# Recurrent mix on one core: the head sums one row further behind, the token sum and the token mix at another row

## The chip, the cores and the metric

The program runs on one core of one Trainium2 chip. The metric is device time in microseconds (us), from launch to end, lower is better. The kernel before takes 2801.14 us, the median of 3 runs (2800.57 to 2802.79).

The program is a chain of eight layers (delta attention, ternary FFN, relative attention, hashed FFN, recurrent mix, low-rank FFN, rotary attention, routed FFN) with a layernorm behind each. The change lies in one of them, the recurrent mix, which takes some 210 us of the span.

## The reference, cut to what matters

The recurrent mix works on 4 batches of 256 tokens in the reference's own shape; the kernel holds the same data as 4 batches of 512 tokens by 128 channels, with a layout of its own. What is computed:

```python
xx  = shifted(x) - x                      # token before, minus token
xxx = x + xx * time_maa_x
m   = tanh(xxx @ time_maa_w1)             # 4 groups of 32
mw, mk, mv, mr = m[f] @ time_maa_w2[f]
xw, xk, xv, xr = (x + xx * (time_maa_f + m_f))
r, k, v = xr @ W_r, xk @ W_k, xv @ W_v
w = time_decay + tanh(xw @ time_decay_w1) @ time_decay_w2
def step(S, (r_t, k_t, v_t, w_t)):        # for each token
    kv = k_t (x) v_t
    y_t = r_t . (S + u * kv)
    return exp(-exp(w_t)) * S + kv, y_t
y = layernorm(y) * ln_g + ln_b
out = y @ W_o
```

The result is added to x, and the program's own layernorm follows.

## The kernel before

Channels lie on the 128 partitions and 512 tokens along the free dimension. There are 4 batches, b = 0 to 3. The state of a head is 16 x 16; its second index is taken apart into HS = 16 passes, here called **rows**: for row j of batch b the kernel scans, along the 512 tokens, the state of all 128 (head, index) pairs against value channel j of their head. The rows of the whole layer are numbered g = 16 b + j, 0 to 63. One row goes through these steps:

- **spread(g)** on TensorE (L922): a 128x512 f32 matmul copies value channel j of each head to the head's partitions, into one of 4 banks of PSUM (g mod 4). It waits for scan g-4, which read that bank last.
- **product(g+1)** and **scan(g)** on VectorE (L1098 and L1106). VectorE issues the product of the next row ahead of the scan of this one.
- **read(g)** on GpSimd (L1065): receptance times state, into one of DEEP = 4 buffers. It waits for sum g-4, which read that buffer last.
- **sum(g)** on TensorE (L929): a matmul that gathers the row into one accumulated bank of PSUM, SUMS, for all 16 rows of the batch. The first sum of a batch (g = 16 b) starts that bank anew, and waits until VectorE has taken the last batch out of it.

TensorE's program is written out by hand: in row j it issues spread(g), then pieces of the next batch's projections and of the last batch's norm, then sum(g - BEHIND), with BEHIND = 3.

Around the rows lie the pieces. For the **next** batch VectorE computes the shifted difference xx and behind it the **token mix** xxx (L1073 and L1075, both in `shift`, row 0). TensorE multiplies it (`tokens_mixed`, L872, row 4), ScalarE takes tanh (L997), TensorE makes the four mixes in two pairs (`first_mixes`, row 6, `later_mixes`, row 8, both L875), VectorE applies them (`scale_mix`, L1079, rows 4 and 6; `add_tokens`, L1083, rows 5, 7 and 8), and TensorE makes values, keys, receptance and decay (L891, L895, L900, L906, L910, L914, rows 10 to 15). For the **last** batch VectorE adds the accumulated sums to a term of its own, the **token sum** (`sum_up`, L1111, row 2), TensorE makes the mean (L935, row 7) and the variance (L939, row 9), VectorE centres and scales (L1116 row 5, L1121 row 9, L1125 row 10), and TensorE and VectorE finish with L945 and L1129 in row 15.

Each engine runs its list in order; semaphores tie the engines together. No DMA and nothing of SyncE's queue takes part in these rows, and no scheduler moves anything: the order is that of the code. The functions below are printed with the line numbers of the profile.

Of the kernel before, what the change touches and what calls it, by code (L numbers as in the profile page):

```python
# [809 lines left out]
def rwkv_attention(c):  # L810
# [4 lines left out]
    d = c.dram  # L815
    HS = 16
    DEEP = 4
    BEHIND = 3
    loaded, chain = c.sem("rw_loaded"), c.sem("rw_chain")
    pe_done, act_done = c.sem("rw_pe"), c.sem("rw_act")  # L820
    spreads, keyed, scanned, read, summed = (c.sem("rw_" + n) for n in ("spreads", "keyed", "scanned", "read", "summed"))
# [1 line left out]
    with ExitStack() as ctx:  # L823
# [41 lines left out]
        def _(eng):  # L865
# [11 lines left out]
            def first_mixes(b):  # L877
                eng.wait_ge(act_done, b * ACTS + 1)
                eng.wait_ge(chain, b * STEPS)
                mix_of(b, 2, 0)  # L880
                mix_of(b, 1, 1)
# [75 lines left out]
            for b in range(B):  # L957
                following, tail = b + 1 < B, b > 0
                for j in range(HS):
                    g = b * HS + j  # L960
                    spread_row(g)
                    if following and j == 4:
                        tokens_mixed(b + 1)
                    if following and j == 6:
                        first_mixes(b + 1)
                    if tail and j == 7:
                        mean(b - 1)
                    if following and j == 8:
                        later_mixes(b + 1)
                    if tail and j == 9:  # L970
                        variance(b - 1)
                    if following and j == 10:
                        values(b + 1)
                    if following and j == 11:
                        keys(b + 1)
                    if following and j == 12:
                        receptance(b + 1)
                        decay_down(b + 1)
                    if following and j == 14:
                        decay_up(b + 1)  # L980
                    if following and j == 15:
                        own_weights(b + 1)
                    if tail and j == 15:
                        output(b - 1)
                    if g >= BEHIND:
                        sums(g - BEHIND)
            for g in range(B * HS - BEHIND, B * HS):
                sums(g)
# [78 lines left out]
        @block.vector  # L1067
        def _(eng):
            def x(b):
                return c.X[:, b, PAD:PAD + T]  # L1070

            def shift(b):
                eng.tensor_tensor(xx[:, :], c.X[:, b, PAD - 1:PAD + T - 1], x(b), ALU.subtract).then_inc(chain, 1)  # L1073
                eng.wait_ge(chain, b * STEPS + 1)
                eng.scalar_tensor_tensor(xxx[:, :], xx[:, :], maa[:, 0:1], x(b), ALU.mult, ALU.add).then_inc(chain, 1)  # L1075

            def scale_mix(b, f, at):
                eng.wait_ge(pe_done, b * PES + at)
                eng.scalar_tensor_tensor(mix[:, f, :], turn(at), maa[:, 1 + f:2 + f], xx[:, :], ALU.add, ALU.mult).then_inc(chain, 1)  # L1079

            def add_tokens(b, f, after):
                eng.wait_ge(chain, b * STEPS + after)
                eng.tensor_tensor(mix[:, f, :], mix[:, f, :], x(b), ALU.add).then_inc(chain, 1)  # L1083

            def own_keys(b):
                eng.wait_ge(act_done, b * ACTS + 4)
                eng.scalar_tensor_tensor(ruk[:, :], rkv[:, b % 2, 2, :], maa[:, 6:7], rkv[:, b % 2, 0, :], ALU.mult, ALU.mult).then_inc(chain, 1)

            def own_values(b):
                eng.wait_ge(pe_done, b * PES + 11)  # L1090
                eng.tensor_tensor(we[:, b % 2, :], rkv[:, b % 2, 1, :], turn(1), ALU.mult).then_inc(chain, 1)

            def products(g):
                b = g // HS
                if g % HS == 0:
                    eng.wait_ge(act_done, b * ACTS + 3)
                eng.wait_ge(spreads, g + 1)
                eng.tensor_tensor(row(g), rkv[:, b % 2, 0, :], row(g), ALU.mult).then_inc(keyed, 1)  # L1098

            def scan(b, j):  # L1100
                g = b * HS + j
                eng.wait_ge(act_done, b * ACTS + 7)
                eng.wait_ge(keyed, g + 1)
                if g >= DEEP:
                    eng.wait_ge(read, g - DEEP + 1)
                eng.tensor_tensor_scan(S[:, j % DEEP, 1:], wd[:, b % 2, :], row(g), 0.0, ALU.mult, ALU.add).then_inc(scanned, 1)  # L1106

            def sum_up(b):
                eng.wait_ge(summed, (b + 1) * HS)
                eng.wait_ge(chain, (b + 1) * STEPS)  # L1110
                eng.tensor_tensor(Y[:, :], we[:, b % 2, :], SUMS, ALU.add).then_inc(yo, 1)  # L1111

            def centre(b):
                eng.wait_ge(ym, b + 1)
                eng.wait_ge(yo, 2 * b + 1)
                eng.tensor_tensor(centred[:, :], Y[:, :], TAIL, ALU.subtract).then_inc(yc, 1)  # L1116

            def scale_norm(b):
                eng.wait_ge(yl, 2 * b + 2)
                eng.wait_ge(yc, b + 1)  # L1120
                eng.scalar_tensor_tensor(own[:, :], centred[:, :], maa[:, 7:8], Q[:, 1, :], ALU.mult, ALU.mult).then_inc(yn, 1)  # L1121

            def shift_norm(b):
                eng.wait_ge(yn, 2 * b + 1)
                eng.tensor_scalar(Y[:, :], own[:, :], maa[:, 8:9], None, ALU.add).then_inc(yn, 1)  # L1125

            def residual(b):
                eng.wait_ge(yr, b + 1)
                eng.tensor_tensor(c.R[:, b, :], x(b), TAIL, ALU.add).then_inc(yo, 1)  # L1129

            for n in range(DEEP):
                eng.memset(S[:, n, 0:1], 0.0)
            eng.wait_ge(loaded, 16 * len(pairs))
            shift(0)
            scale_mix(0, 2, 2)
            scale_mix(0, 1, 3)
            add_tokens(0, 2, 3)
            scale_mix(0, 3, 4)
            scale_mix(0, 0, 5)
            add_tokens(0, 1, 4)  # L1140
            add_tokens(0, 3, 6)
            add_tokens(0, 0, 7)
            own_keys(0)
            own_values(0)
            products(0)
            for b in range(B):
                following, tail = b + 1 < B, b > 0
                for j in range(HS):
                    if b * HS + j + 1 < B * HS:
                        products(b * HS + j + 1)  # L1150
                    scan(b, j)
                    if following and j == 0:
                        shift(b + 1)
                    if tail and j == 2:
                        sum_up(b - 1)
                    if following and j == 4:
                        scale_mix(b + 1, 2, 2)
                        scale_mix(b + 1, 1, 3)
                    if tail and j == 5:
                        centre(b - 1)  # L1160
                    if following and j == 5:
                        add_tokens(b + 1, 2, 3)
                    if following and j == 6:
                        scale_mix(b + 1, 3, 4)
                        scale_mix(b + 1, 0, 5)
                    if following and j == 7:
                        add_tokens(b + 1, 1, 4)
                        add_tokens(b + 1, 3, 6)
                    if following and j == 8:
                        add_tokens(b + 1, 0, 7)  # L1170
                    if tail and j == 9:
                        scale_norm(b - 1)
                    if tail and j == 10:
                        shift_norm(b - 1)
                    if following and j == 12:
                        own_keys(b + 1)
                    if tail and j == 15:
                        residual(b - 1)
                    if following and j == 15:
                        own_values(b + 1)  # L1180
            sum_up(B - 1)
            centre(B - 1)
            scale_norm(B - 1)
            shift_norm(B - 1)
            residual(B - 1)
# [462 lines left out]
def relative_attention(c):  # L1648
# [23 lines left out]
    LAST = NITER * QT  # L1672
    AHEAD, BEHIND, STAGES, RING = 5, 2, 3, 6
    LEAD = AHEAD * QUAD
# [29 lines left out]
    with ExitStack() as ctx:  # L1704
# [120 lines left out]
        def _(eng):  # L1825
# [79 lines left out]
            for j in range(AHEAD):  # L1905
                write_bands(j)
                if j == 0:
                    pack(1)
                elif j <= AHEAD - BEHIND:
                    read_windows(j - 1)  # L1910
# [4 lines left out]
            for j in range(LAST):  # L1915
                m, t = j // QT, j % QT
                if j + AHEAD - BEHIND < LAST:
                    read_windows(j + AHEAD - BEHIND)
# [1318 lines left out]
```

## Time and profile before

| what | value |
|---|---|
| median of 3 runs | 2801.14 us (2800.57 to 2802.79) |
| the profiled execution's own time | 2805.52 us |
| its span | 2803.7 us |
| mean granted TensorE clock | 0.94 |
| TensorE matmul busy over the span | 2424.5 us (86%) |
| VectorE busy over the span | 2077.3 us (74%) |
| ScalarE busy | 1585.5 us (57%) |
| GpSimd busy | 269.5 us (10%) |

The rows of the recurrent mix run from 2126.9 to 2301.3 us of the span, with some 20 us of first projections ahead and a tail behind. "Idle before" in the rows further down is the time in which an engine had nothing running ahead of an instruction, with the instruction that ended the wait. An instruction of VectorE starts some 0.1 us before the profile shows the end of the one ahead of it, so distances from start to start are a little shorter than durations.

### The profile page before, as it was taken

The page shows a single profiled execution, that of the slowest core. Times are in us where ns is not written, and L with a number is a line of the kernel's source. Part 1 is how long each engine was busy: PE and PEld are TensorE (multiplying, and loading weights), DVE is VectorE, ACT ScalarE, POOL GpSimd, SP SyncE. Part 2 cuts the span into 40 slices and gives each one's busy share as a digit, 9 for nine tenths or more (in the row PEclk, how much of TensorE's full clock was granted, in tenths as well). Part 3 has the DMA queues.
Part 4 walks back from the last instruction along what each step waited for, and adds up shares of the span by engine and source line. Part 5 has one row for each costly group of instructions (what it writes and reads, how often), then busy time and mean ns, then how long its engine had stood idle before and what let it go on. Part 6 is the DMA issues. An engine that isn't in the chain of part 4 may idle for free. (4 is left out here: it accounts for less than half of the span.)

```text
span 2803.7 us, 64145 instructions
## 1 busy us (share of the span) xinstructions
PE 2424.5 (86%) x25861; PEld 1600.8 (57%) x25861; DVE 2077.3 (74%) x3811; ACT 1585.5 (57%) x4086; POOL 269.5 (10%) x278
## 2 busy tenths in 40 slices
PE   6888888888888888888994999999998887999777
PEld 5666676666666676674442666666642332332376
DVE  6899898899999989892124777788727775886465
ACT  3566666666667666665334777777641113667344
POOL 0000000000000000000011101100003342110342
PEclk9999999999999999999996999999999998999889
DMA  5111111110111111002007998999510003220421
GB/s 188 32 33 25 25 32 33 32 32 18 32 32 33 33 32 32 17 17 72 0 12 198 229 250 227 229 244 236 130 37 2 0 0 108 70 74 20 176 70 65
DMA packets 205727, 219.50 MB, mean 78 GB/s; under 512 B 32966, under 2 KB 191446, under 8 KB 199990
## 3 DMA queue, kind: packets, MB, share of 16 engines
q1 hardware_dynamic: 202400, 209.59, 28.5%
q0 software_dynamic: 2400, 4.95, 0.5%
q8 instruction: 207, 3.39, 0.5%
q10 hardware_dynamic: 633, 0.85, 0.1%
q14 instruction: 87, 0.71, 0.1%
HBM read 137.96 MB, written 79.79 MB: 78 GB/s over the span
## 5 line engine op out<-in xcount | busy, mean ns | idle before, releaser
L3003 DVE TENSOR_REDUCE dl_ZO<-dl_XP 128x64 f32<-128x128 f32 (+6 forms) x448 | 219.7, 491 | 15.4
L2116 ACT ACTIVATE da_AB<-ps 128x384 f32<-128x384 f32 x256 | 124.7, 491 | 137.7 <-PE ps L1963 134.1
L2578 PE MATMUL ps<-dl_ST,ident 128*128 128x512 f32 x416 | 187.8, 595 | 0.0
L2998 DVE TENSOR_TENSOR dl_XP<-dl_ZO,dl_G 128x128 f32<-128x128 f32 (+5 forms) x384 | 177.1, 461 | 13.2
L1596 DVE TENSOR_REDUCE ra_top<-ps 128x1 f32<-128x512 f32 x256 | 159.2, 680 | 36.1 <-PE ps L1362 35.2
L2126 ACT ACTIVATE da_E<-ps,da_top 128x512 f32<-128x512 f32 x256 | 176.2, 688 | 15.3 <-DVE da_top L2273 14.8
L2270 DVE TENSOR_TENSOR ps<-ps,da_window 128x192 f32<-128x192 f32 (+1 forms) x256 | 101.2, 395 | 111.5 <-PE ps L1986 107.2
L2273 DVE TENSOR_REDUCE da_top<-ps 128x1 f32<-128x512 f32 x256 | 177.0, 691 | 8.8
L1496 ACT ACTIVATE ra_PT<-ps 128x512 f32<-128x512 f32 x256 | 136.0, 601 | 61.0 <-PE ps L1393 60.7
L1993 PE MATMUL ps<-ident,da_E 128*128 128x128 f32 x1024 | 168.7, 288 | 1.3 <-ACT da_E L2126 1.3
L2512 PEld LDWEIGHTS ps<-X,dl_taps_v 128*128 128x128 f32 x1088 | 140.3, 210 | 16.6 <-issue 10.9
L1727 POOL MEMSET da_K<- 32x4096 f32 x2 | 7.0, 3506 | 1456.6 <-POOLq L195 1456.6
L2512 PE MATMUL ps<-X,dl_taps_v 128*128 128x128 f32 x1088 | 142.8, 293 | 4.5 <-DVE dl_taps_v L3061 4.5
L1993 PEld LDWEIGHTS ps<-ident,da_E 128*128 128x128 f32 x1024 | 108.2, 141 | 50.3 <-issue 39.3
L2808 ACT ACTIVATE dl_bv<-dl_Wb,dl_beta_now 128x32 f32<-128x32 f32 x512 | 112.9, 335 | 41.3 <-DVE dl_Wb L2895 39.6
L2816 ACT ACTIVATE dl_FB<-dl_F,dl_beta_now 128x32 f32<-128x32 f32 x512 | 126.8, 350 | 4.0 <-DVE dl_F L2900 2.9
L2512 PE MATMUL ps<-X,dl_taps_q 128*128 128x128 f32 x1088 | 125.9, 274 | 0.0
L2512 PE MATMUL ps<-X,dl_taps_k 128*128 128x128 f32 x1088 | 124.2, 273 | 0.0
L2785 ACT ACTIVATE dl_WT<-ps 128x256 f32<-128x256 f32 x64 | 21.1, 381 | 181.3 <-PE ps L2601 181.3
L2512 PEld LDWEIGHTS ps<-X,dl_taps_q 128*128 128x128 f32 x1088 | 122.8, 191 | 1.1
L2512 PEld LDWEIGHTS ps<-X,dl_taps_k 128*128 128x128 f32 x1088 | 122.8, 191 | 0.0
L2578 PEld LDWEIGHTS ps<-dl_ST,ident 128*128 128x128 f32 x416 | 74.6, 190 | 78.7 <-issue 71.7
(416 smaller groups left out, 5932.2 us busy)
## 6 DMA issues: line engine op xcount, KB each, us to landing
da_bands<-da_AB SPq DMA_DIRECT2D x128, 384.0 KB, 3.8
dl_Abc<-dl_ends SPq DMA_DIRECT2D x64, 512.0 KB, 6.3
da_window<-da_bands SPq DMA_DIRECT2D x128, 192.0 KB, 4.4
da_across<-da_bands SPq DMA_DIRECT2D x128, 192.0 KB, 4.4
da_parts<-da_split SPq DMA_DIRECT2D x64, 96.0 KB, 3.4
ra_parts<-ra_split SPq DMA_DIRECT2D x16, 384.0 KB, 3.7
rf_We<-in_rf_We SPq DMA_DIRECT2D x1, 4608.0 KB, 22.8
da_K<-da_parts SPq DMA_DIRECT2D x16, 256.0 KB
```

Of the source, the lines that this page charges most:

```text
L1496: eng.activation(PT[:, k % 2, h, :], ps[:, tscore_bank(UNITS * m + v), :], ACT.Exp).then_inc(s["exps"], 1)
L1596: eng.tensor_reduce(top[:, m % 2, u:u + 1], ps[:, score_bank(UNITS * m + u), :], AXX, ALU.max, negate=True).then_inc(s["maxima"], 1)
L1993: mm = eng.transpose(ps[:, 2 + U % 2, k * P:(k + 1) * P], E[:, U % 2, k * P:(k + 1) * P], c.ident[:, :])
L2116: eng.activation(AB[:, j % STAGES, h, :, :], ps[:, band_bank(v), 0:2 * BAND].rearrange("p (k x) -> p k x", k=2), ACT.Copy)\
L2126: eng.activation(E[:, U % 2, :], ps[:, score_bank(U), :], ACT.Exp, bias=top[:, u:u + 1], accum_out=total[:, m % 2, u:u + 1]).then_inc(s["e ...
L2273: eng.tensor_reduce(top[:, u:u + 1], bank, AXX, ALU.max, negate=True).then_inc(s["maxima"], 1)
L2512: mm = eng.matmul(out, taps[w][:, tap, cols], columns_of(c.X, m, tap), start=tap == 0, stop=tap == TAPS - 1)
L2578: eng.matmul(ps[:, UPDATES[r], :], c.ident[:, :], quarters[:, r, :, :], start=True, stop=alone)
L2808: ins = eng.activation(bv[:, e, :, t], values[:, t, :], ACT.Copy, scale=beta_now[:, 0, t:t + 1])
L2816: ins = eng.activation(FB[:, e, :, t // SB, t % SB], F[:, e, :, t // SB, t % SB], ACT.Copy, scale=beta_now[:, 1, t:t + 1])
L2998: link(eng.tensor_tensor(XP[:, :, :, SB - t:], seen.unsqueeze(1).to_broadcast([P, 2, I, t + 1]), G[:, x:x + 2, keys][:, ::-1, :].unsqueeze ...
L3003: link(eng.tensor_reduce(ZO[:, to:to + 1 + (2 * I - 1) * CH:CH].rearrange("p (k i) -> p k i", k=2), XP[:, :, :, SB - 1 - t:], AXX, ALU.add))
```

## The change

BEHIND goes from 3 to 4: in row j TensorE now issues sum(g-4) where it issued sum(g-3). The pieces `tokens_mixed`, `first_mixes`, `mean`, `later_mixes` and `variance` go one row later on TensorE; those of rows 10 to 15 stay. On VectorE the token mix is split off from the shifted difference and issued in row 1, and the token sum goes from row 2 to row 1, ahead of the token mix. No instruction is added or taken out.

```diff
-    BEHIND = 3
+    BEHIND = 4
...
                     spread_row(g)
-                    if following and j == 4:
+                    if following and j == 5:
                         tokens_mixed(b + 1)
-                    if following and j == 6:
+                    if following and j == 7:
                         first_mixes(b + 1)
-                    if tail and j == 7:
+                    if tail and j == 8:
                         mean(b - 1)
-                    if following and j == 8:
+                    if following and j == 9:
                         later_mixes(b + 1)
-                    if tail and j == 9:
+                    if tail and j == 10:
                         variance(b - 1)
                     if following and j == 10:
                         values(b + 1)
...
             def shift(b):
                 eng.tensor_tensor(xx[:, :], c.X[:, b, PAD - 1:PAD + T - 1], x(b), ALU.subtract).then_inc(chain, 1)
+
+            def mix_tokens(b):
                 eng.wait_ge(chain, b * STEPS + 1)
                 eng.scalar_tensor_tensor(xxx[:, :], xx[:, :], maa[:, 0:1], x(b), ALU.mult, ALU.add).then_inc(chain, 1)
...
             shift(0)
+            mix_tokens(0)
...
                     if following and j == 0:
                         shift(b + 1)
-                    if tail and j == 2:
+                    if tail and j == 1:
                         sum_up(b - 1)
+                    if following and j == 1:
+                        mix_tokens(b + 1)
```

TensorE at the start of batch 0, from its first spreads on (L922 is a spread, L929 a sum, L872 the tokens' product), before:

```order
L922 MATMUL ps<-rw_rkv,rw_spread 128x512 x4
L929 MATMUL ps<-rw_rS,rw_gather 128x512
L922 MATMUL ps<-rw_rkv,rw_spread 128x512
L872 MATMUL ps<-rw_xxx,rw_w 128x512
L929 MATMUL ps<-rw_rS,rw_gather 128x512
```

and changed:

```order
L922 MATMUL ps<-rw_rkv,rw_spread 128x512 x5
L929 MATMUL ps<-rw_rS,rw_gather 128x512
L922 MATMUL ps<-rw_rkv,rw_spread 128x512
L872 MATMUL ps<-rw_xxx,rw_w 128x512
L929 MATMUL ps<-rw_rS,rw_gather 128x512
```

Five spreads stand ahead of the first sum instead of four. From there on the list reads alike up to the middle of the batch, with every spread one row further on than its neighbours: the tokens' product, which stood behind spread 4, stands behind spread 5.

TensorE in the middle of batch 1, from the mean (L935) by the later mixes (L875) and the variance (L939) to the values (L891), before:

```order
L935 MATMUL ps<-rw_Y,ones_mean 128x512
L929 MATMUL ps<-rw_rS,rw_gather 128x512
L922 MATMUL ps<-rw_rkv,rw_spread 128x512
L875 MATMUL ps<-rw_m,rw_w 128x512 x2
L929 MATMUL ps<-rw_rS,rw_gather 128x512
L922 MATMUL ps<-rw_rkv,rw_spread 128x512
L939 MATMUL ps<-rw_Q,ones_mean 128x512
L929 MATMUL ps<-rw_rS,rw_gather 128x512
L922 MATMUL ps<-rw_rkv,rw_spread 128x512
L891 MATMUL ps<-rw_mix,rw_Wrkv 128x512
```

and changed:

```order
L935 MATMUL ps<-rw_Y,ones_mean 128x512
L929 MATMUL ps<-rw_rS,rw_gather 128x512
L922 MATMUL ps<-rw_rkv,rw_spread 128x512
L875 MATMUL ps<-rw_m,rw_w 128x512 x2
L929 MATMUL ps<-rw_rS,rw_gather 128x512
L922 MATMUL ps<-rw_rkv,rw_spread 128x512
L939 MATMUL ps<-rw_Q,ones_mean 128x512
L891 MATMUL ps<-rw_mix,rw_Wrkv 128x512
```

The variance and the values now stand in one row, with no sum and no spread between them.

VectorE where batch 1 begins, from the shifted difference (L1073) on, before:

```order
L1073 TENSOR_TENSOR rw_xx<-X 128x512
L1075 SCALAR_TENSOR_TENSOR rw_xxx<-rw_xx,rw_maa,X 128x512
L1098 TENSOR_TENSOR ps<-rw_rkv,ps 128x512
L1106 SCALAR_TENSOR_TENSOR rw_S<-rw_wd,ps 128x512
L1098 TENSOR_TENSOR ps<-rw_rkv,ps 128x512
L1106 SCALAR_TENSOR_TENSOR rw_S<-rw_wd,ps 128x512
L1111 TENSOR_TENSOR rw_Y<-rw_we,ps 128x512
L1098 TENSOR_TENSOR ps<-rw_rkv,ps 128x512
```

and changed, where L1100 is the product, L1108 the scan, L1113 the token sum and L1077 the token mix:

```order
L1073 TENSOR_TENSOR rw_xx<-X 128x512
L1100 TENSOR_TENSOR ps<-rw_rkv,ps 128x512
L1108 SCALAR_TENSOR_TENSOR rw_S<-rw_wd,ps 128x512
L1113 TENSOR_TENSOR rw_Y<-rw_we,ps 128x512
L1077 SCALAR_TENSOR_TENSOR rw_xxx<-rw_xx,rw_maa,X 128x512
L1100 TENSOR_TENSOR ps<-rw_rkv,ps 128x512
```

One product and one scan (row 1) stand between the difference and the token sum now, where it was two of each and the token mix; the token mix comes behind the token sum. GpSimd's and ScalarE's lists keep their order.

## Rows read from the trace of the kernel before

**Rows 1.** Windows: length; busy PE, PEld, DVE, ACT, POOL; granted clock; DMA share, GB/s.
```profile
2126.90:2168.40 41.50, 37.04 (x85) 13.76 (x83) 37.36 (x45) 4.30 (x7) 20.08 (x16) 1.00 0.00 0
2168.40:2187.00 18.60, 13.41 (x27) 5.15 (x26) 12.40 (x15) 0.60 (x1) 6.63 (x6) 0.82 0.00 0
2187.00:2218.60 31.60, 29.90 (x69) 11.60 (x68) 28.65 (x36) 8.21 (x11) 14.37 (x11) 1.00 0.00 1
2218.60:2237.60 19.00, 13.22 (x25) 5.11 (x25) 12.28 (x15) 0.60 (x1) 6.29 (x5) 0.82 0.00 0
...
2269.20:2301.30 32.10, 27.95 (x62) 11.13 (x62) 28.89 (x35) 3.23 (x4) 17.84 (x15) 1.00 0.00 1
```
**Rows 2.** Waits, 2103 to 2316: us in total, times, longest us.
```profile
DVE ps L1098 <- PE ps L922: 22.5, 16, 3.9
...
PE ps L929 <- DVE rw_Y L1111: 14.5, 3, 5.8
```
**Rows 3.** Timeline of VectorE where batch 1 begins: start, us, instruction [idle before].
```profile
2168.44 1.22 DVE L1106 TENSOR_TENSOR_SCAN rw_S<-rw_wd,ps 128x512 f32<-128x512 f32 x1
...
2170.27 1.63 DVE L1075 SCALAR_TENSOR_TENSOR rw_xxx<-rw_xx,rw_maa,X 128x512 f32<-128x512 f32 x1
...
2173.55 0.67 DVE L1098 TENSOR_TENSOR ps<-rw_rkv,ps 128x512 f32<-128x512 f32 x1
2174.13 1.20 DVE L1106 TENSOR_TENSOR_SCAN rw_S<-rw_wd,ps 128x512 f32<-128x512 f32 x1
2175.26 0.65 DVE L1111 TENSOR_TENSOR rw_Y<-rw_we,ps 128x512 f32<-128x512 f32 x1
2179.78 0.70 DVE L1098 TENSOR_TENSOR ps<-rw_rkv,ps 128x512 f32<-128x512 f32 x1 [3.87 <-PE ps L922]
...
2185.72 1.41 DVE L1079 SCALAR_TENSOR_TENSOR rw_mix<-ps,rw_maa,rw_xx 128x512 f32<-128x512 f32 x2 [0.95 <-PE ps L875]
```
**Rows 4.** Timeline of TensorE's matmuls, from the last sum of batch 0.
```profile
2168.80 1.12 PE L929 MATMUL ps<-rw_rS,rw_gather 128*128 128x512 f32 x2
2169.76 1.02 PE L922 MATMUL ps<-rw_rkv,rw_spread 128*128 128x512 f32 x2
2175.97 2.07 PE L929 MATMUL ps<-rw_rS,rw_gather 128*128 128x512 f32 x2 [5.18 <-DVE rw_Y L1111]
2177.84 1.91 PE L922 MATMUL ps<-rw_rkv,rw_spread 128*128 128x512 f32 x2
...
2181.03 1.02 PE L929 MATMUL ps<-rw_rS,rw_gather 128*128 128x512 f32 x2
```
**Rows 5.** One window behind that stop, columns as in rows 1.
```profile
2176.00:2178.00 2.00, 2.00 (x3) 0.96 (x4) 0.00 (x0) 0.00 (x0) 0.56 (x1) 0.50 0.00 0
```
**Rows 6.** Timeline at batch 0's end, VectorE and TensorE.
```profile
2158.20 0.70 DVE L1098 TENSOR_TENSOR ps<-rw_rkv,ps 128x512 f32<-128x512 f32 x1 [1.83 <-PE ps L922]
...
2164.40 1.02 PE L922 MATMUL ps<-rw_rkv,rw_spread 128*128 128x512 f32 x2
...
2165.26 1.02 PE L929 MATMUL ps<-rw_rS,rw_gather 128*128 128x512 f32 x2
...
2165.53 0.70 DVE L1098 TENSOR_TENSOR ps<-rw_rkv,ps 128x512 f32<-128x512 f32 x1 [0.83 <-PE ps L922]
```
**Rows 7.** The token mix alone: durations ns min/median/max, first and last start.
```profile
L1075 DVE SCALAR_TENSOR_TENSOR rw_xxx<-rw_xx,rw_maa,X x4: 753/1632/1633, 2106.5 to 2220.4; 128x512 f32<-128x512 f32 x4
```
**Rows 8.** Timeline, VectorE and GpSimd side by side.
```profile
2150.56 0.66 DVE L1083 TENSOR_TENSOR rw_mix<-rw_mix,X 128x512 f32<-128x512 f32 x1
...
2150.77 1.57 POOL L1065 TENSOR_TENSOR rw_rS<-rw_rkv,rw_S 128x512 f32<-128x512 f32 x1 [2.41 <-DVE rw_S L1106]
...
2175.47 1.09 POOL L1065 TENSOR_TENSOR rw_rS<-rw_rkv,rw_S 128x512 f32<-128x512 f32 x1 [0.61 <-DVE rw_S L1106]
```
**Rows 9.** Timeline, TensorE and VectorE where batch 3 begins.
```profile
2274.56 1.12 PE L929 MATMUL ps<-rw_rS,rw_gather 128*128 128x512 f32 x2 [3.51 <-DVE rw_Y L1111]
...
2282.73 0.69 DVE L1116 TENSOR_TENSOR rw_centred<-rw_Y,ps 128x512 f32<-128x512 f32 x1 [0.90 <-PE ps L935]
```

## The prediction

> **What bounds the kernel now.** I read the windows of the layer's rows first, then who waited for whom, then the timelines of VectorE and TensorE side by side at the two places where VectorE stands still. Between 2126.9 and 2301.3 us VectorE is the engine that sets the pace: no other runs a list as full without waiting for it. What it idles is length less busy in [rows 1]: 4.1 us in batch 0, 6.2 at the start of batch 1, 3.0 in its rest, 6.7 at the start of batch 2, and 3.2 in the last window; the rest of batch 2, not shown, repeats the 3.0 of batch 1. Together 26.2 us, and that is all that reordering can give back, apart from contention. By [rows 2] 22.5 us of the layer's idle time are products that wait for a spread.
>
> The largest piece is at a batch's start. Behind scan 16 VectorE does the difference, the token mix, scans 17 and 18, and only then, at 2175.26, the token sum [rows 3]. TensorE had the last sum of batch 0 out at 2168.80 and spread 19 at 2169.76, then stood for 5.18 us, because the first sum of batch 1 may not start before the token sum [rows 4]. Spread 20 is queued behind that sum, so product 20 waits 3.87 us in its turn [rows 3]. The stop also costs clock: the granted clock behind it is 0.50 [rows 5], TensorE's 1.2 GHz level, and sum, spread and tokens' product take from 2175.97 to 2181.03, 5.1 us, where the full-rate distances of 0.96 and 0.86 [rows 4, 6] would make 2.7. Three such stops cost 14.5 us of TensorE [rows 2]. The one at batch 3 is 3.51 us long [rows 9], and its window keeps a clock of 1.00 [rows 1].
>
> The second piece is at a batch's end. A row costs VectorE 0.58 + 1.13 = 1.71 us (product to scan, scan to the next) [rows 3], and TensorE 0.86 for a spread [rows 6] and 0.86 to 0.96 for a sum [rows 4]. They are level, so in rows 10 to 15, where TensorE has six or seven pieces and VectorE two to five short ones, products wait: 1.83 and 0.83 us at batch 0's end [rows 6].
>
> **The change, part by part.** Nothing is added or removed; each spread goes ahead of one sum, and the token sum comes earlier. Times below are followed, with these distances: spread's start to its product's start 1.13 [rows 6], scan's start to its read's start 1.34, the read 1.09 to 1.57 [rows 3, 8], then the sum 0.06 behind what releases it [rows 3, 4]. From a scan's end to the spread it releases I take 0.5; its floor is that 0.06.
>
> *Batch starts.* Row 1 now puts the token sum at scan 16 + 1.13 + 0.59 (difference) + 0.58 + 1.13 = scan 16 + 3.4, where it was + 6.8 [rows 3]. It needs sum 15. With the earlier spreads TensorE is at spread 19 when scan 16 starts plus 1.1, sum 15 starts at + 2.0 and is to be read at + 3.1: just in time, with 0.3 to spare (0.9 in batch 2, by the same walk). Spread 20 now stands ahead of the sum that waits, so TensorE has it out by + 3.7, and sum 16 goes at + 4.2: a stop of 0.4 to 1 us in place of 5.18. Product 20 comes at + 7.3 and waits for nothing. What is late next is the first mixes: they follow spread 7 of the batch, which needs scan 3's end (1.71 + 1.21 = 2.9 behind scan 2's start) and sum 2 (1.34 + 1.09 + 0.06 + 0.86 = 3.35); before they followed spread 6 behind the same sum 2. So the 0.95 us of [rows 3] stays. Idle at the starts of batches 1 and 2 goes from 6.2 and 6.7 to 0.9 each: **11.1 us**.
>
> *Batch 3's start* has no next batch. The token sum comes at + 2.8, sum 48 at + 3.6, spread 52 is ahead of it. The mean is late instead: it follows spread 56, which scan 52 releases, and the centring waits some 1.3 us where it waited 0.90 [rows 9]. Idle goes from 3.2 to 1.3: **1.9 us**.
>
> *Batch ends.* Let S be the start of spread 12. Up to spread 16 TensorE has receptance, decay down, sum 8, spread 13, sum 9, spread 14, decay up, sum 10, spread 15, own weights, sum 11: 11 us at 0.86 to 1.05, and product 16 may start at S + 12.1. Scan 8, which releases spread 12, started at S - 1.7; scan 9 is 2.31 on (one addition), three rows bring scan 12 to S + 5.7, the 0.65 of L1087 and two rows scan 14 to S + 9.8, product 16 to S + 10.95. The wait is 1.15, or 0.95 as idle (VectorE starts 0.08 before the end ahead of it), where batch 0 had 3.2. Before, S itself was late, since spread 12 stood behind sum 8, which waits for a read; that is the sum which is now behind it. In batches 1 and 2 TensorE has one piece more and VectorE 1.0 us more: S + 13.0 against S + 12.0, idle 0.9 where it was 3.0. In batch 0 the later mixes, now behind spread 9, come 0.3 after VectorE (scan 5's end + 0.5 + 0.96 + 1.16, against 2.2), and the first mixes 0.15 later. Batch 0 keeps 0.95 + 1.1 + 0.3 = 2.35 of its 4.1, batches 1 and 2 0.9 of 3.0: **1.8 + 2 x 2.1 = 6.0 us**.
>
> *The token mix.* Its median is 1632 ns and its minimum 753 [rows 7]: in the three slow cases GpSimd's read is under way when it starts. An addition that starts 0.21 ahead of GpSimd's read takes 0.66, and the read 1.57 instead [rows 8]. In batch 0 the token mix now follows scan 1 directly, as that addition follows its scan, and starts before the read: 0.75 in place of 1.63, **0.9 us**. In batches 1 and 2 the token sum puts it 0.4 behind the read's start, so it costs what it cost. The ends are 0 and 0.9 in batch 0 (plus or minus 0.9 in the others); I take 0.9, since the read's 1.34 delay is steady. The Trainium skill, SBUF — State Buffer, section "SBUF: two separate sides", has the shared port pair of VectorE and GpSimd as an exclusive lock, taken by whoever starts first: by it the two placements would also differ as I take them, and the batches 1 and 2 mix would end about 1.1 + 0.7 behind the read's start, 0.1 us less than in rows 7, nothing for the sum.
>
> *Pieces moved at no cost.* Variance: one row later, the scaling in row 9 had several us to spare in batches 1 and 2 and has 1.3 left in batch 3. Values lie one piece further back, in ScalarE's idle time. The read waits for sum g-4, issued some 3 us before it is needed even in row 15.
>
> *Overlap.* 22 waits become 9, and each wait gone gives 0.08 more, since starts overlap ends: **1.0 us**.
>
> **Sum:** 11.1 + 1.9 + 6.0 + 0.9 + 1.0 = 20.9 us. The profiled execution took 2805.5, its span 2803.7, so it would be 2784.6; the runs' median stands 4.4 lower, 2801.1, and gives **2780.2 us**.
>
> **Rivals.**
> 1. *Only the stops go.* If TensorE's pieces, not the order, set the batch ends, the 6.0 stay and part of the overlap: gain 14.3, 2786.8. For it: TensorE's busy share there is 29.90 of 31.60 [rows 1]. Against: it would have to be late by its whole list, and the walk finds only 1 us.
> 2. *The clock falls all the same* at the starts of batches 1 and 2, since TensorE still pauses there: 2 x (5.1 - 2.7) = 4.8 back, 2785.0. For: it did fall in those two windows [rows 1]. Against: a stop of 3.51 left it whole.
> 3. *The wait moves to the token sum.* If sum 15 comes 4 us later than walked, VectorE stands at row 1 instead of at product 20. The sums are one further behind, and the margin is 0.3. The starts would give little and the ends some 2: 2798. Against: TensorE's list up to sum 15 holds one spread more than before, 0.86 us, while the token sum comes 3.4 earlier than scan 18 allowed and sum 15 was out 6.5 before it.
> 4. *Slower.* TensorE's many short pauses, each spread now held by the scan four rows back, keep it at 1.2 GHz. A sum and a spread then take 1.87 + 1.70 or so, about 1.8 more than a row has. It would decide from 12 rows on (20.9 / 1.8); with the first eight rows of three batches it is 24 x 1.8 - 20.9 = + 22, 2823. Against: in batch 0 and in the ends such pauses leave the clock at 1.00 [rows 1]. The Trainium skill's page TensorE: Matmul & The Clock Gate, section "A second HAM failure mode: psum-queue depth-cycling", has frequent short idles between matmul groups making the gate swing; by that rule this case would be the outcome. No row here shows it.
>
> **How the numbers follow.** Chances: forecast 0.70, rival 1 0.10, rival 2 0.08, rival 3 0.07, rival 4 0.05. The forecast's own range is 2777 to 2785: the 0.5 against 0.06, the token mix, and 1 us per place of the walk. Rivals 1 and 2 reach to 2788, and I go to 2790 for half of rival 3's wait; 2776 below. A measurement of this kernel can tell some 0.2%, 5.6 us, from no change: the forecast and rivals 1 and 2 are faster, most of rival 3 is the same: 0.90 faster, 0.05 same, 0.05 slower.
>
> **What would show it.** In the profile after: TensorE's wait on the token sum (14.5 us) under 3; the granted clock 1.00 in all these windows; products waiting for spreads under 5 us in total, from 22.5; the three or so waits for first mixes still about 1 us each; batch 0's token mix at 0.75; the layer's rows some 21 us shorter, nothing else moved. The forecast is wrong if the token sum waits for the last sum by more than a microsecond, or if the clock is at 0.50 anywhere between 2130 and 2280.

## The result and the profile after

The changed kernel takes 2778.71 us, the median of 4 runs (2770.59 to 2781.19), beside 2801.77 (4 runs) for the kernel before on the same chip. The ratio is 0.9913, 95% interval 0.9898 to 0.9928: 20 to 29 us faster, 24.4 at the middle. Measured twice more, beside other kernels, the changed kernel had ratios of 0.9901 (0.9870 to 0.9932) and 0.9908 (0.9878 to 0.9939). The prediction was 2780.2.

The profiled execution is the fastest of the four, with a span of 2768.8 us where the one before had 2803.7. Not all of those 34.9 us are the change's: the last write of the layernorm ahead of the layer (L126) starts at 2104.69 before and 2093.18 after, so 11.5 us lie in code that is the same. Below, **the layer** is the time from the start of that write to the start of the layer's last residual add (L1129, now L1131): 209.6 us before (2104.69 to 2314.29), 186.1 after (2093.18 to 2279.27), 23.5 less. It is a far steadier measure than the whole: the two other profiled executions of the changed kernel have 185.8 and 185.9. There is one profile of the kernel before.

The windows that answer to [rows 1], cut at the same instructions (length; busy PE, PEld, DVE, ACT, POOL; granted clock; DMA share; GB/s):

```profile
2115.60:2153.70 38.10, 35.88 (x83) 13.68 (x82) 36.27 (x45) 4.29 (x7) 20.45 (x16) 1.00 0.00 0
2153.70:2166.50 12.80, 12.49 (x31) 4.91 (x30) 11.72 (x15) 0.60 (x1) 6.61 (x6) 1.00 0.00 0
2166.50:2195.50 29.00, 28.14 (x65) 11.01 (x64) 28.39 (x36) 8.10 (x11) 14.35 (x11) 1.00 0.00 1
2195.50:2208.40 12.90, 11.99 (x30) 4.71 (x29) 11.82 (x15) 0.60 (x1) 6.29 (x5) 1.00 0.00 0
2208.40:2237.40 29.00, 28.14 (x65) 10.99 (x64) 28.39 (x36) 8.10 (x11) 14.34 (x11) 1.00 0.00 0
2237.40:2267.20 29.80, 28.55 (x64) 11.37 (x62) 28.57 (x36) 3.23 (x4) 17.89 (x15) 1.00 0.00 1
```

Length less VectorE's busy time is its idle time, in the order of the rows: 1.8, 1.1, 0.6, 1.1, 0.6 and 1.2 us, together 6.4 where [rows 1] had 26.2. The two starts shrink from 18.6 and 19.0 us to 12.8 and 12.9, and their clock is 1.00 where it was 0.82. All six windows make 151.6 us against 174.4.

VectorE's waits in them (us in total, times, longest us), which answer to [rows 2]; these rows are cut to the windows above, where the kernel before has 22.5 for the products as well:

```profile
DVE rw_mix L1081 <- PE ps L875: 3.2, 3, 1.1
DVE ps L1100 <- PE ps L922: 2.0, 3, 0.8
DVE rw_centred L1118 <- PE ps L935: 1.2, 1, 1.2
```

and TensorE's wait on the token sum in the same stretch:

```profile
PE ps L929 <- DVE rw_Y L1113: 1.5, 3, 0.9
```

Products wait 2.0 us where they waited 22.5, and TensorE 1.5 where it waited 14.5; the first mixes (L1081) and the mean of batch 3 (L1118) are most of what is late now, as the prediction had it.

VectorE's timeline where batch 1 begins (start, us, instruction, [idle before]) answers to [rows 3]:

```profile
2153.72 1.22 DVE L1108 TENSOR_TENSOR_SCAN rw_S<-rw_wd,ps 128x512 f32<-128x512 f32 x1
...
2157.16 0.66 DVE L1113 TENSOR_TENSOR rw_Y<-rw_we,ps 128x512 f32<-128x512 f32 x1
2157.74 1.27 DVE L1077 SCALAR_TENSOR_TENSOR rw_xxx<-rw_xx,rw_maa,X 128x512 f32<-128x512 f32 x1
...
2165.24 1.41 DVE L1081 SCALAR_TENSOR_TENSOR rw_mix<-ps,rw_maa,rw_xx 128x512 f32<-128x512 f32 x2 [1.08 <-PE ps L875]
```

and TensorE's to [rows 4]:

```profile
2155.68 1.02 PE L929 MATMUL ps<-rw_rS,rw_gather 128*128 128x512 f32 x2
2156.54 1.02 PE L922 MATMUL ps<-rw_rkv,rw_spread 128*128 128x512 f32 x2
2157.87 1.12 PE L929 MATMUL ps<-rw_rS,rw_gather 128*128 128x512 f32 x2 [0.31 <-DVE rw_Y L1113]
```

The token sum comes 3.44 us behind scan 16, for the 3.4 walked; the last sum of batch 0 at + 1.96 (2.0 walked), spread 20 at + 2.8, the first sum of batch 1 at + 4.15 (4.2). The stop is 0.31 us; the one at batch 2 is 0.91. The read of GpSimd starts 0.21 us behind the token sum and is not stretched:

```profile
2157.37 1.09 POOL L1065 TENSOR_TENSOR rw_rS<-rw_rkv,rw_S 128x512 f32<-128x512 f32 x1 [0.73 <-DVE rw_S L1108]
```

An addition with the same lead stretches it to 1.57 [rows 8], and so did the difference that stood here before (2169.57, the read 2169.78). The token sum has one of its two inputs in PSUM; the other two have both in SBUF.

### The profile page after: what moved, and what is told of

It reads as the page before. It is cut to its first block and busy times, and to the rows that moved or that the text cites. A ratio compares the mean times of both kernels' runs of the same rounds, so it can differ in the third digit from the quotient of the medians.

```text
span 2768.8 us, 64093 instructions
## 1 busy us (share of the span) xinstructions
PE 2399.0 (87%) x25809; PEld 1586.9 (57%) x25861; DVE 2073.2 (75%) x3811; ACT 1583.8 (57%) x4086; POOL 269.6 (10%) x278
## 5 line engine op out<-in xcount | busy, mean ns | idle before, releaser
L2517 PEld LDWEIGHTS ps<-X,dl_taps_v 128*128 128x128 f32 x1088 | 133.6, 201 | 15.3 <-issue 11.7
L2517 PE MATMUL ps<-X,dl_taps_v 128*128 128x128 f32 x1088 | 135.8, 284 | 2.4 <-DVE dl_taps_v L3066 2.4
## 6 DMA issues: line engine op xcount, KB each, us to landing
rf_We<-in_rf_We SPq DMA_DIRECT2D x1, 4608.0 KB, 22.8
```

Source lines behind the costliest of these rows:

```text
L2517: mm = eng.matmul(out, taps[w][:, tap, cols], columns_of(c.X, m, tap), start=tap == 0, stop=tap == TAPS - 1)
```

## The experiments

The table gives the distances between starts of scans on VectorE, in us: scan 0 to 16 is batch 0, 16 to 21 and 32 to 37 the starts of batches 1 and 2, 21 to 32 and 37 to 48 their rests, 48 to 54 the start of batch 3. The edits are told against the kernel named in each.

| kernel | 0-16 | 16-21 | 21-32 | 32-37 | 37-48 | 48-54 | layer |
|---|---|---|---|---|---|---|---|
| before | 41.53 | 19.20 | 30.97 | 19.71 | 30.98 | 14.63 | 209.6 |
| changed | 38.10 | 13.44 | 28.41 | 13.44 | 28.42 | 12.78 | 186.1 |
| tensor part alone | 39.51 | 18.52 | 28.42 | 18.52 | 28.41 | 16.20 | 200.6 |
| vector part alone | 40.59 | 13.45 | 30.98 | 13.44 | 30.98 | 12.93 | 194.0 |
| changed, pieces early | 37.37 | 12.92 | 28.74 | 14.62 | 28.74 | 11.44 | 185.1 |
| before, stop filled | 41.53 | 16.82 | 30.98 | 16.82 | 30.98 | 16.27 | 205.9 |
| changed, mix first | 38.09 | 14.11 | 28.41 | 14.11 | 28.42 | 12.78 | 187.0 |
| pieces early, mix first | 37.56 | 11.79 | 28.74 | 11.80 | 28.74 | 11.44 | 182.2 |
| changed, five behind | 37.85 | 13.73 | 28.42 | 13.13 | 28.42 | 13.27 | 186.0 |

**Tensor part alone.** In the changed kernel:

```diff
                     if following and j == 0:
                         shift(b + 1)
-                    if tail and j == 1:
+                        mix_tokens(b + 1)
+                    if tail and j == 2:
                         sum_up(b - 1)
-                    if following and j == 1:
-                        mix_tokens(b + 1)
```

> TensorE's part alone (sums four rows behind, early pieces one row later), VectorE's list as before. The layer, from the last write of the layernorm ahead of it to its own last residual add, took 209.6 us before and 186.0 changed. Theory (each part removes its own waits): the batch ends gain in full (6 us), batch 3's start too (2 us), and at the starts of batches 1 and 2 spread 20 goes ahead of the sum that waits, so product 20 waits for nothing, but TensorE still stands some 4 us on the token sum and the first mixes come 3 us late instead of 1: some 2.5 us of 5.7 gained each. Layer about 196 to 197. Rival (the order on TensorE is all that matters): layer 187. Rival (the token sum's place is all that matters): layer 203, the batch ends only.

Measured: ratio to before 0.9967 (0.9953 to 0.9981), layer 200.6. The batch ends gain in full. The starts of batches 1 and 2 give 0.7 and 1.2 us, not 2.5, and batch 3's start, where I expected 2 us of gain, takes 1.6 us more (16.20 for 14.63). The layer misses the 196 to 197 expected by 4 us. Start of batch 1, TensorE and then VectorE:

```profile
2163.01 2.02 PE L929 MATMUL ps<-rw_rS,rw_gather 128*128 128x512 f32 x2 [3.69 <-DVE rw_Y L1113]
2164.82 1.86 PE L922 MATMUL ps<-rw_rkv,rw_spread 128*128 128x512 f32 x2
```
```profile
2166.73 0.70 DVE L1100 TENSOR_TENSOR ps<-rw_rkv,ps 128x512 f32<-128x512 f32 x1 [2.05 <-PE ps L922]
2167.33 1.22 DVE L1108 TENSOR_TENSOR_SCAN rw_S<-rw_wd,ps 128x512 f32<-128x512 f32 x1
2172.07 1.41 DVE L1081 SCALAR_TENSOR_TENSOR rw_mix<-ps,rw_maa,rw_xx 128x512 f32<-128x512 f32 x2 [3.52 <-PE ps L875]
```
```profile
2163.00:2165.00 2.00, 1.99 (x3) 0.96 (x4) 1.68 (x2) 0.00 (x0) 0.79 (x2) 0.52 0.00 0
```

Product 20 waits for nothing, as expected, but product 21 and the first mixes pay instead, and behind the stop of 3.69 us the granted clock is 0.52. The same happens at batch 3, behind a stop of 2.02 us:

```profile
2254.61 1.48 PE L929 MATMUL ps<-rw_rS,rw_gather 128*128 128x512 f32 x2 [2.02 <-DVE rw_Y L1113]
```
```profile
2254.00:2257.00 3.00, 2.39 (x4) 1.13 (x5) 2.28 (x3) 0.00 (x0) 1.68 (x2) 0.71 0.02 5
```

There the next product waits 1.55 us and the centring 2.47. So the waits moved as expected, and the expectation had no fall of the clock in its price. How much each of the three starts would gain at a full clock, no run shows.

**Vector part alone.** In the changed kernel:

```diff
-    BEHIND = 4
+    BEHIND = 3
...
-                    if following and j == 5:
+                    if following and j == 4:
                         tokens_mixed(b + 1)
```

and likewise `first_mixes` at 6, `mean` at 7, `later_mixes` at 8, `variance` at 9.

> VectorE's part alone (token sum in row 1, token mix behind it), TensorE's list as before with the sums three rows behind. Theory: the stops at the starts of batches 1 and 2 fall from 5.2 and 5.8 us to about 2, too short for the clock to fall, and product 20 waits for nothing: 5.7 us gained each; batch 3's start 1.5, the token mix of batch 0 0.9; the batch ends keep their 3 us of waits each. Layer about 195. Together with the tensor part alone that is more than the whole change gains, since both remove part of the same stops. Rival (the order on TensorE is all that matters): layer above 203.

Measured: ratio 0.9951 (0.9935 to 0.9966), layer 194.0. The stops:

```profile
2165.59 1.13 PE L929 MATMUL ps<-rw_rS,rw_gather 128*128 128x512 f32 x2 [1.81 <-DVE rw_Y L1113]
...
2210.01 1.12 PE L929 MATMUL ps<-rw_rS,rw_gather 128*128 128x512 f32 x2 [2.41 <-DVE rw_Y L1113]
```

Both starts are 13.45 and 13.44 us, those of the changed kernel; both ends are 30.98, those of the kernel before. So the starts belong to VectorE's edit and the ends to TensorE's. Alone they give 15.6 and 9.0 us, 24.6 together, where the whole change gives 23.5. From scan 0 to scan 54 it is 14.7 and 7.4, 22.1 together for 22.4; the rest is the layer's tail, from scan 54 on, which is shorter in all three (29.22 us for the vector part, 28.78 for the tensor part and 29.06 for both, where it had 30.36) and so is counted twice in the 24.6. Both stops at batches 1 and 2 left the clock at 1.00:

```profile
2165.00:2170.00 5.00, 4.41 (x11) 2.02 (x12) 5.00 (x6) 0.60 (x1) 2.18 (x2) 1.00 0.00 0
2210.00:2214.00 4.00, 3.99 (x10) 1.82 (x10) 4.00 (x5) 0.60 (x1) 1.59 (x2) 1.00 0.00 0
```

**Pieces early.** The changed kernel with the five rows of TensorE's pieces as in the diff above, and BEHIND left at 4.

> The changed kernel with TensorE's five early pieces back at their old rows (4, 6, 7, 8, 9); the sums stay four behind and VectorE's list stays changed. Theory: the first mixes and the mean come one spread and sum (1.8 us) earlier against VectorE, so the waits of 1.0 us for the first mixes in three batches and of 1.2 for the mean of batch 3 go nearly whole; the tokens' product stands a row earlier and TensorE waits up to 1.6 us for the token mix. Layer 182 to 184, 2 to 4 us less than the changed kernel. Rival (the pieces had to move, else TensorE stands on the token mix and the clock falls): layer 188 or more.

Measured: ratio 0.9920 (0.9891 to 0.9950), layer 185.1. TensorE now waits for the token mix; at batch 2:

```profile
2210.20 1.87 PE L872 MATMUL ps<-rw_xxx,rw_w 128*128 128x512 f32 x2 [2.10 <-DVE rw_xxx L1077]
2211.86 1.92 PE L929 MATMUL ps<-rw_rS,rw_gather 128*128 128x512 f32 x2
```
```profile
2210.00:2213.00 3.00, 2.80 (x4) 1.26 (x5) 3.00 (x5) 0.60 (x1) 0.99 (x1) 0.57 0.00 0
```

Behind that pause of 2.10 us the clock is 0.57, and batch 2's start takes 14.62 us where batch 1's, with a pause of 1.50 and a full clock, takes 12.92. Batch 3's start falls to 11.44, since its mean is in time. The first mixes still wait up to 0.9. Half of each theory, and short of the 182 to 184 expected: the early pieces gain 0.5 to 1.3 a place, the clock takes 1.7 back, and the rests of batches 1 and 2 lose 0.3 each (28.74 for 28.4).

**Stop filled.** In the kernel before:

```diff
                 b, j = g // HS, g % HS
+                if j == 0 and b in (1, 2):
+                    for _ in range(5):
+                        eng.matmul(turn(0), spread[:, 0, :], rkv[:, b % 2, 1, :], start=True, stop=True)
```

> The kernel before, with five more 128x512 f32 matmuls (4.3 us) into an unused bank of PSUM on TensorE ahead of the first sum of batches 1 and 2, where it stood 5.2 and 5.8 us: they keep the engine busy and change nothing else (their result is used by nothing). Prices the clock alone. Theory: granted clock 1.00 behind both places, sum, spread and tokens' product take 2.7 us instead of 5.1, so the layer loses 4 to 5 us: about 205. Rival (the clock costs nothing, since VectorE waits for the token sum in any case): layer 209.6.

Measured: ratio 0.9987 (0.9972 to 1.0001), which does not tell it from 1; layer 205.9. The starts of batches 1 and 2 take 2.4 and 2.9 us less, at a clock of 1.00: that is what the clock alone cost there, of the 5.8 and 6.3 us that the change gained. (The fill leaves 0.90 and 1.50 us of the two stops.) The unedited stop at batch 3 was the surprise:

```profile
2261.26 1.91 PE L932 MATMUL ps<-rw_rS,rw_gather 128*128 128x512 f32 x2 [3.51 <-DVE rw_Y L1114]
2262.96 1.91 PE L922 MATMUL ps<-rw_rkv,rw_spread 128*128 128x512 f32 x2
```
```profile
2260.00:2265.00 5.00, 3.74 (x5) 1.63 (x6) 1.29 (x3) 0.00 (x0) 1.23 (x2) 0.66 0.00 0
```

It is the stop of [rows 9], 3.51 us to the hundredth, which kept the full clock there and loses it here; batch 3's start costs 1.6 us more (16.27 for 14.63), and for that the layer lies above the 205 expected.

**Mix first.** In the changed kernel:

```diff
-                    if tail and j == 1:
-                        sum_up(b - 1)
                     if following and j == 1:
                         mix_tokens(b + 1)
+                    if tail and j == 1:
+                        sum_up(b - 1)
```

> The changed kernel with the token mix ahead of the token sum in row 1, so that it starts 0.2 us before GpSimd's read instead of 0.4 behind it. Theory (behind the token sum TensorE works without a pause up to the first mixes, so its list sets the start of the batch): the token mix falls from 1.27 to 0.75 us, but the token sum, and all of TensorE's list behind it, comes 0.6 us later, and VectorE waits 1.7 us for the first mixes instead of 1.1: scan 16 to scan 21 takes 13.9 to 14.1 instead of 13.4, the layer 187.3 where the changed kernel has 186.1. Rival (VectorE's own list sets the start, as in the prediction's sum): 12.9 from scan 16 to 21, layer 185.0.

Measured: ratio 0.9914 (0.9883 to 0.9944), layer 187.0, scan 16 to 21 in 14.11. VectorE:

```profile
2166.48 0.73 DVE L1077 SCALAR_TENSOR_TENSOR rw_xxx<-rw_xx,rw_maa,X 128x512 f32<-128x512 f32 x1
...
2175.23 1.41 DVE L1081 SCALAR_TENSOR_TENSOR rw_mix<-ps,rw_maa,rw_xx 128x512 f32<-128x512 f32 x2 [2.27 <-PE ps L875]
```

The token mix gets its 0.73 us, and the start gets 0.7 longer: from the token sum to the first mixes TensorE's list sets the pace in the changed kernel, and what VectorE saves there it waits for. This is the theory's 13.9 to 14.1, not the rival's 12.9: the prediction's sum, which counts what VectorE's list saves as gained, would have had it wrong here.

**Pieces early, mix first.** Both edits in one.

> Both edits: TensorE's early pieces at their old rows, and the token mix ahead of the token sum. With the pieces early alone, TensorE stood 1.5 and 2.1 us on the token mix, and in batch 2 the clock fell behind the 2.1; the layer took 185.1. Theory: the token mix now ends 1.2 us earlier, TensorE's pause on it falls under 0.6, the token sum is ready when TensorE comes to the first sum of the batch, and the first mixes are there before VectorE: scan 16 to scan 21 about 11.7 us (13.4 in the changed kernel), layer 181 to 182. Rival (the clock falls behind any pause of that kind, or the first mixes are bound by tanh on ScalarE): layer 185 or more.

Measured: ratio 0.9899 (0.9868 to 0.9930), layer 182.2, starts 11.79 and 11.80. TensorE at batch 1:

```profile
2160.69 1.12 PE L872 MATMUL ps<-rw_xxx,rw_w 128*128 128x512 f32 x2 [0.38 <-DVE rw_xxx L1077]
```

One edit gains 1.0 us alone, the other loses 0.9, and together they gain 3.9 in this profile, since the first needs the token mix early. In batch 2 the pause was 0.97, more than the 0.6 expected, and in batch 0, where there is no token sum to go ahead of, it stayed at 1.83.

**Five behind.** `BEHIND = 5` in the changed kernel.

> The changed kernel with the sums five rows behind. The prediction's rival 3 by its own mechanism: the last sum of a batch now stands behind spread 20, which needs scan 16's end, so it is to be read 3.7 us or more after scan 16 started, and the token sum is issued at 3.4. Theory: VectorE waits 0.3 to 1 us at each token sum, the batch ends gain at most 0.9 each, layer 185 to 187.5. Rival (one row further behind is another step of the same gain): no wait at the token sum, layer below 184.5.

Measured: ratio 0.9906 (0.9873 to 0.9940), layer 186.0. At batch 1:

```profile
2161.91 1.22 DVE L1108 TENSOR_TENSOR_SCAN rw_S<-rw_wd,ps 128x512 f32<-128x512 f32 x1
2164.35 0.69 DVE L1113 TENSOR_TENSOR rw_Y<-rw_we,ps 128x512 f32<-128x512 f32 x1 [1.22 <-PE ps L929]
2164.96 0.75 DVE L1077 SCALAR_TENSOR_TENSOR rw_xxx<-rw_xx,rw_maa,X 128x512 f32<-128x512 f32 x1
```

Rival 3's mechanism, at a size of its own: the token sum waits 1.22 us for the last sum (up to 1 expected), 3.1 over the three batch starts, and the ends gain nothing more (28.42). The first mixes wait less in turn, 1.9 us in all for 3.2, so the layer is the changed kernel's within 0.1 us. With the token sum in row 1 a fifth row behind brings nothing.

**The changed kernel again.**

> The changed kernel once more, for a second profiled execution. In the first one 11.5 of the 35 us between the profiled spans lay ahead of the changed layer, in code that is the same. Theory (the granted clock falls at other places of the first layer from one execution to the next): the layer takes 186.1 again within 0.2, while the code ahead of it ends somewhere else between 2090 and 2106 us. Rival (the change reached the code ahead of it too): it ends at 2093 us again.

Measured: layer 185.8. The last write of the layernorm ahead, first in the changed kernel's first profile, then in this one:

```profile
2093.18 0.69 DVE L126 TENSOR_TENSOR X<-ln_D,ln_Q 128x512 f32<-128x512 f32 x1 [0.54 <-ACT ln_Q L138]
```
```profile
2102.98 0.69 DVE L126 TENSOR_TENSOR X<-ln_D,ln_Q 128x512 f32<-128x512 f32 x1 [0.54 <-ACT ln_Q L138]
```

The same program reaches this point 9.8 us apart, nearly as far as the 11.5 between before and after. So the 11.5 need be no effect of the change; the stop-filled kernel, with the same code there, has 2096.70. That the granted clock in the first layer (0.94 and 0.93 over its 1290 us in the two) makes the difference would fit, but was not tested.

**Changed, and pieces early with mix first, in five rounds.**

> The changed kernel beside the next one, both in five rounds on one chip, since three rounds could not tell them apart. Theory: ratio to the kernel before 0.991 to 0.992, layer 186.

> The version with TensorE's early pieces at their old rows and the token mix ahead of the token sum, beside the changed kernel. Theory: 3.6 to 3.9 us less than the changed kernel, all of it in the layer (182.2): ratio to before 0.990. Rival: the layer is shorter only in the one execution profiled so far, and the medians are equal.

Measured: ratios 0.9908 (0.9878 to 0.9939) and 0.9908 (0.9877 to 0.9939), medians 2776.76 and 2777.27. The layer: 185.9, and 185.4 where the same kernel had 182.2. TensorE in the second kernel's batch 0, and a window there:

```profile
2123.66 2.03 PE L872 MATMUL ps<-rw_xxx,rw_w 128*128 128x512 f32 x2 [1.82 <-DVE rw_xxx L1077]
```
```profile
2123.00:2126.00 3.00, 2.34 (x3) 1.14 (x4) 3.00 (x5) 0.27 (x1) 1.97 (x2) 0.62 0.00 0
```

In the first profile the same pause was 1.83 us and its window stayed at 1.00. Here the clock fell behind it, and batch 0 took 39.26 instead of 37.56 us (another 1.5 lay in the first projections, also at a lower clock). So the starts of batches 1 and 2 are 1.65 us shorter each in both profiles, but in one of the two half of that went again in batch 0. The expected 3.6 to 3.9 us are not there, the medians are equal as the rival had it, and I cannot call this kernel faster than the changed one.

## Why the prediction was right

*Starts of batches 1 and 2*, forecast 11.1 us of idle time: 10.8. The idle left is 1.1 each for 0.9, all of it the first mixes, as said. The experiments divide it: VectorE's edit alone gives all of it, and 2.4 and 2.9 us of what a start took before were the clock (the filled stop).

*Batch 3's start* and its rest, 1.9: 2.0. The mean is what is late (1.23 for 1.3).

*Batch ends*, 6.0: 7.0. Here one term was mis-sized. I let a spread start 0.5 us behind the scan that releases it. VectorE and TensorE in batch 0:

```profile
2137.28 1.21 DVE L1108 TENSOR_TENSOR_SCAN rw_S<-rw_wd,ps 128x512 f32<-128x512 f32 x1
...
2138.54 1.12 PE L922 MATMUL ps<-rw_rkv,rw_spread 128*128 128x512 f32 x2 [1.00 <-DVE rw_S L1108]
...
2150.81 0.70 DVE L1100 TENSOR_TENSOR ps<-rw_rkv,ps 128x512 f32<-128x512 f32 x1 [0.81 <-PE ps L922]
```

The scan (scan 8) ends at 2138.49 and spread 12 starts 0.05 behind it: the floor that I had named and not taken. So TensorE's list starts 0.45 us earlier against VectorE's than walked. The rest of the walk holds: product 16 starts at spread 12 + 12.27 (12.1 walked), and it takes the only wait in batch 0's rows behind the first mixes, 0.81 us instead of 0.95; the ends of batches 1 and 2 keep 0.61 for 0.9; and the later mixes, which I had 0.3 late, are in time. The tensor part alone shows these ends by themselves, 28.42.

*The token mix*, 0.9 in batch 0: it takes 0.73 there. I had it unchanged in batches 1 and 2 and it fell from 1.63 to 1.27. GpSimd's read was 1.57 us long there before, held up by the difference; now it runs 2157.37 to 2158.46, and the mix ends 0.55 behind the read's end, as it did before. What I missed was that the read would be shorter. It is worth 0.7 us. The Trainium skill, SBUF — State Buffer, section "SBUF: two separate sides", has the pair as an exclusive lock for the whole instruction of whoever starts first. The order of the two fits that, but the 0.55 us is less than the 0.73 to 0.75 that the mix takes by itself; and the prediction's own working from it, 1.1 + 0.7 behind the read's start, makes a mix of 1.4 us with a start 0.4 behind, 0.2 under the 1.63 of [rows 7] and not 0.1. It measured 1.27.

*Overlap*, 1.0: the prediction's count of 22 waits and 9 was off; by the waits of VectorE in these windows it is 20 (16 products, three first mixes, one centring) and 7, so the difference of 13 stands. VectorE's busy time in the windows fell by 3.1 us; 0.9 and 0.7 are the mix, so about 1.5 is left for this, of which some 0.3 is that the 62 products are a little shorter in sum.

The six windows gained 22.8 us for the 20.9 of the sum: the ends were forecast 1.0 too low, the mix 0.7 and the overlap 0.5, the starts 0.3 too high. The layer gained 23.5; the 0.7 more come from the variance of batch 3, behind the rows, which fell on a full clock (1.13 us) where it had taken 2.08. The forecast had nothing for that, so towards its number it is luck. It is no accident of one execution, though: all three profiled executions of the changed kernel have 1.13, and both of the kernel with pieces early and mix first have 2.07 or 2.08, behind the same wait of 1.44 us. What decides it was not tested.

*The rivals.* Only the stops: the ends gained 7.0. The clock falls all the same: 1.00 in all windows, and the layer within 0.3 us in three profiles. But my evidence against it was weak: the 3.51 us stop that kept its clock lost it in the stop-filled kernel, and the tensor part alone lost it behind 2.02. The changed kernel's longest stop on the token sum is 0.91 us. That this is what protects it is argued: 1.57 us (mix first) and 1.81 and 2.41 (vector part alone) kept the clock too, and no run shows from what length on it is at risk. Wait moves to the token sum: true only from five rows on. Slower: no trace of it. The Trainium skill's page TensorE: Matmul & The Clock Gate, section "A second HAM failure mode: psum-queue depth-cycling", tells of a kernel whose frequent short idles between groups made the gate swing; with pauses up to 1.0 us between matmuls, no window of the changed kernel's rows from 2115.60 to 2267.20 shows that.

## What to carry to other kernels

Where one in-order engine waits for a hand-over of another, ask both what is queued behind the waiting instruction and what is queued ahead of the releasing one; here moving one instruction of VectorE up by 3.4 us took away a stop, its queue and the clock loss behind it, while putting one more independent matmul ahead of the wait, with the stop left at 3.69 us, gave 0.7 and 1.2 us and cost 1.6 at a third place, clock losses included. When two engines are level, an order that lets one run a row ahead pays wherever extra pieces make it late (here 2.3 us a batch), until the hand-over itself depends on what was put off. Judge a change of 1% by the layer's own time in the trace, where the whole program scatters by 10 us in code that is not touched.

## What the runs showed of the hardware

- The same stop of TensorE does not always cost clock: 3.51 us left it at 1.00 in one kernel's execution and brought it to 0.66 over a window in another; 1.83 and 1.82 us in one and the same kernel did nothing once and gave 0.62 the other time; 2.02 and 2.10 brought it down and 2.41 did not. Each fall that could be priced cost the rows behind it 1.6 to 2.9 us.
- In these rows a matmul whose engine is idle and whose last semaphore comes from VectorE starts 0.05 to 0.06 us behind the end of the instruction that releases it (spread 12 at 2138.54 behind scan 8's end at 2138.49).
- An addition, difference or mix of VectorE with two SBUF inputs that starts 0.2 us ahead of GpSimd's multiply is not slowed (0.66 to 0.73 us) and stretches the multiply from 1.09 us to between 1.44 and 1.58; a mix that starts while the multiply runs ends 0.55 us behind the multiply's end. The token sum, with one input in PSUM, starts 0.21 ahead and stretches nothing (1.09).
